# Filling the gap in front of a block's fourth channel with a convolution piece and six down matmuls

## What is computed

```python
def reference(x, itok, ...):            # x: (B=128, C=32, L=512)
    y = irfft(rfft(x, 2 * L) * rfft(K, 2 * L))[..., :L] + x * D[:, None]   # K: one kernel of length L per channel
    y = y * (arange(L) < length)                                           # mask
    q = fp8(clip(y / in_scale, -448, 448))
    hidden = silu(q @ gate_w.T * s) * (q @ up_w.T * s)                     # I = 1376
    return x + fp8(clip(hidden / down_scale)) @ down_w.T * s
```

## Time and profile before

| | us |
|---|---|
| median of 3 runs (lowest, highest) | 334.01 (332.64, 334.09) |
| the profiled execution, its own time | 333.13 |
| its span in the profile | 331.4 |
| PE busy | 310.4 (94%) |
| DVE busy | 304.5 (92%) |
| ACT busy | 205.4 (62%) |

### The profile page before, as it was taken

One profiled execution on the slowest core, in us unless ns is written; L12 is line 12 of the kernel. 1 busy time (PEld: TensorE's weight loads), 2 busy tenths in 40 slices (PEclk: granted clock), 3 DMA queues, 4 the chain that ended last, 5 costly groups with the idle time before them and its releaser, 6 DMA issues.

```text
span 331.4 us, 4869 instructions
## 1 busy us (share of the span) xinstructions
PE 310.4 (94%) x1591; PEld 163.6 (49%) x1591; DVE 304.5 (92%) x470; ACT 205.4 (62%) x312; POOL 13.0 (4%) x20
## 2 busy tenths in 40 slices
PE   0879898879999999999999999999999999989996
PEld 0746554445546454555546454555546454434443
DVE  5989899999999899998999899998999899997784
ACT  2457778366764958475764957475764958544540
POOL 2022000000001000010000000010001000010010
PEclk9999999999999999999999999999999999999999
DMA  6559999500000782046600791046600760070027
GB/s 240 101 165 216 236 289 370 197 1 2 0 0 0 130 287 93 2 74 207 225 0 0 127 342 38 0 79 205 224 0 1 130 253 0 0 129 0 0 37 220
DMA packets 13794, 38.27 MB, mean 115 GB/s; under 512 B 1392, under 2 KB 6352, under 8 KB 10832
## 3 DMA queue, kind: packets, MB, share of 16 engines
q1 hardware_dynamic: 8192, 26.48, 22.5%
q0 software_dynamic: 5584, 11.57, 20.0%
HBM read 33.80 MB, written 15.81 MB: 150 GB/s over the span
## 4 chain that ended last, share of the span: by engine, by line
PE 81%; DVE 12%; issue 2%; DMA 2%; ACT 2%; DVEq 0%; SPq 0%
PE gate_ps L490 20%; PE up_ps L490 20%; PE down_ps L456 19%; PE y_ps L441 17%; DVE yt L773 2%; DVE hv L800 2%; DVE ht L808 2%; PE y_ps L423 2%; DVE hq L817 2%; PE y_ps L534 1%; DVE yq L784 1%; DVE ym L765 1%; PE down_ps L534 1%; DMA toep<-kpad_scratch 1%; DMA prm<-in_params 1%
## 5 line engine op out<-in xcount | busy, mean ns | idle before, releaser
L366 ACT ACTIVATE sil<-gate_ps,fac 128x512 f32<-128x512 f32 (+1 forms) x88 | 60.1, 685 | 86.8 <-PE gate_ps L490 86.5
L490 PE MATMUL gate_ps<-yq,wg 128*128 128x512 bf16 (+2 forms) x372 | 89.5, 363 | 5.9 <-DVE yq L791 2.9
L490 PE MATMUL up_ps<-yq,wu 128*128 128x512 bf16 (+2 forms) x372 | 89.5, 363 | 0.0
L441 PE MATMUL y_ps<-xt,toep 128*128 128x512 f32 (+3 forms) x256 | 80.7, 435 | 0.7 <-DMA toep<-kpad_scratch 0.7
L800 DVE SCALAR_TENSOR_TENSOR hv<-up_ps,fac,sil 128x512 f32<-128x512 f32 (+1 forms) x88 | 65.6, 746 | 15.7 <-ACT sil L366 11.5
L456 PE MATMUL down_ps<-wd,hq 128*128 128x512 bf16 (+1 forms) x308 | 79.2, 379 | 0.3 <-DVE hq L825 0.3
L490 PEld LDWEIGHTS gate_ps<-yq,wg 128*128 128x128 bf16 x372 | 35.8, 100 | 48.5 <-issue 4.6
L441 PEld LDWEIGHTS y_ps<-xt,toep 128*128 128x128 f32 x256 | 47.0, 190 | 21.1 <-issue 2.9
L490 PEld LDWEIGHTS up_ps<-yq,wu 128*128 128x128 bf16 x372 | 36.3, 100 | 38.3
L808 DVE SCALAR_TENSOR_TENSOR ht<-hc,hv 128x1024 f32<-128x1024 f32 (+1 forms) x48 | 54.1, 1127 | 0.0
L817 DVE SCALAR_TENSOR_TENSOR hq<-hc,ht 128x1024 bf16<-128x1024 f32 (+1 forms) x48 | 54.1, 1126 | 0.0
(11 more groups left out here) (139 smaller groups left out, 110.7 us busy)
## 6 DMA issues: line engine op xcount, KB each, us to landing
xt<-in_xT SPq DMA_DIRECT2D x8, 1024.0 KB, 7.4
toep<-kpad_scratch SPq DMA_DIRECT2D x7, 1024.0 KB, 9.7
out<-in_x SPq DMA_DIRECT2D x7, 1024.0 KB, 5.7
out<-res POOLq DMA_DIRECT2D x7, 1024.0 KB, 8.0
wd<-in_down POOLq DMA_DIRECT2D x1, 1280.0 KB, 25.3
toep<-kpad_scratch SPq DMA_DIRECT2D x4, 256.0 KB, 3.7
xt<-in_x SPq DMA_DIRECT2D x1, 1024.0 KB, 7.2
out<-xt SPq DMA_DIRECT2D x3, 256.0 KB, 3.2
```

Of the source, the lines that this page charges most:

```text
L366: nc.scalar.activation(sil[b][0:w, :], gate_ps[b][0:w, :], ACT.Silu, scale=fac[0:w, S_GATE:S_GATE + 1]).then_inc(silu_done, 1)
L441: last = nc.tensor.matmul(y_ps[h % 2][:, d * P:L], toep[par][:, h, d * P:(d + 1) * P], xt[par][:, h, 0:L - d * P], start=(d == 0), stop=(d ...
L490: mm = nc.tensor.matmul(ps[b][0:w, cols], wt[:, k, c * P:c * P + w], yq[par][:, version, k, cols], start=(k == 0), stop=(k == LB - 1))
```

## The change

In slot 0 the convolution piece (channel 1 of the next block, distance 2) and the down matmuls now stand between the first three channels' gate and up and the fourth's. Slot 0 issues six down matmuls in place of four; slots 1 to 8 four each, slots 9 and 10 three each. The list of DVE, of ACT and of the DMA queues is unchanged.

```diff
-                for s in range(HB * c, HB * (c + 1)):
+                for s in range(DOWN_PLAN[c], DOWN_PLAN[c + 1]):
...
+            def conv_part(g, par, half, c, down, ahead):
+
+                for step, h, distances in CONV_PLAN.get(c, ()):
+                    if step <= ahead and (down or (step, h) != (1, 1)):
+                        conv(g + step, (par + step) % 2, half + (1 if step == 2 else par), h, distances)
...
                         for lo, hi in (((0, HB - 1), (HB - 1, HB)) if c == 0 else ((0, HB),)):
+                            if c == 0 and hi == HB:
+                                conv_part(g, par, half, c, down, ahead)
+                                if down:
+                                    down_part(g - 1, 1 - par, c)
                             if c == 0:
                                 at_least(pe, yq_ready, HB * g + hi)
...
-                    for step, h, distances in CONV_PLAN.get(c, ()):
-                        if step <= ahead and (down or (step, h) != (1, 1)):
-                            conv(g + step, (par + step) % 2, half + (1 if step == 2 else par), h, distances)
-                    if down:
+                    if c or not down:
+                        conv_part(g, par, half, c, down, ahead)
+                    if c and down:
                         down_part(g - 1, 1 - par, c)
...
+DOWN_PLAN = [0, 6, 10, 14, 18, 22, 26, 30, 34, 38, 41, 44]
```

## The result

The change made the kernel slower, and by more than forecast: 359.49 us median (6 runs, 357.37 to 362.22) against 333.44 us (6 runs, 332.39 to 334.10), a ratio of 1.079 (95% interval 1.073 to 1.085), where 349.3 us and a range of 343 to 354 had been forecast. The profiled execution took 358.24 us, with a span of 356.6.

The account below looks back on a forecast made before the run. PE was taken as the bound, DVE close behind. New waits for pair 4's clip, summed over blocks 1 to 7, added 16.2 us to the profiled 333.13 us, giving 349.3 us, range 343 to 354.

Parts of the forecast that it names:

- What bounds the kernel, and that two waits for `yq` were to be gained: PE bounds the kernel; gate's two waits for `yq`, in blocks 1 and 7, could be filled, worth up to 2.9 us.
- The fourth channel 1.79 us late, the product and the clips with it: Block 2, slot 0: fourth channel starts at 108.59, not 106.80; DVE's product moves to 109.92, pair 4's clip to 114.18.
- The wait for pair 4 in slot 1: k = 8, moved from slot 2 to slot 1, waits for DVE's clip of pair 4: 2.60 us in block 2.
- The lower bound, DVE not delayed, 340.8 us: Rival: clip not delayed, k = 8 waits 0.81 us, blocks 2 to 6 cost 4.5 us; chance 0.10.
- by the row at 1.67 us each wait costs only itself: PE ran at full clock after block 1's 1.67 us wait, so new waits were taken to slow no matmuls.
- half rate after 9.13 us: At the start, PE's first matmuls after 9.13 us idle took 5.31 us, 1.78 ns a column.
- The rule of the Trainium skill named there: Idle gaps between bursts of matmuls can put PE's clock back to half each time, slowing the matmuls behind each wait.
- The chance of 0.06: Chance given to the rival that PE's clock falls after each wait, 368 us in all.
- that rival: PE's clock falls after each of seven waits, 2.65 us each, 18.6 us, 368 us in all; chance 0.06.
- reads full in every slice: PE's granted clock row showed full clock throughout the kernel before, although its first matmuls ran slowly.

Follow-up runs that it names:

- the order alone: Changed kernel with four down matmuls in every slot, new order of slot 0 kept, k = 8 in slot 2: 331.53 us, ratio 0.994 to the kernel before.
- the wait filled: Changed kernel with 11 more matmuls of 512 columns right before k = 8 in each block, result overwritten: 349.92 us, ratio 1.049 to the kernel before.
- the plan alone: Changed kernel with convolution piece and down matmuls back behind the fourth channel, changed DOWN_PLAN kept: 341.95 us, ratio 1.023 to the kernel before.
- the order alone's second measurement: Same kernel again, new order of slot 0 with four down matmuls in every slot: 331.92 us, ratio 0.995 to the kernel before.

## Why the prediction was wrong

- *What bounds the kernel, and that two waits for `yq` were to be gained:* right. Both vanished, and the order alone gained 1.2 us.
- *The fourth channel 1.79 us late, the product and the clips with it:* right. In block 2 the product started 4.36 us after the block's start (112.28 in the trace after), 1.73 later than in the earlier trace rows, the clips at 116.54, 8.62 after it where they had been at 6.89.
- *The wait for pair 4 in slot 1:* right in place and size. 2.44 us against 2.60, 2.25 against 2.41, 3.05 against 3.3, seven waits of 17.7 us in all where some 19 were forecast. Its consequences were forecast at 16.2 us and came to 15.9 in the kernel with the wait filled, right block by block. (Its median of 349.92 us next to the forecast 349.3 is closer than it should be read: three of its four runs hold a half-clock stretch, and the one at full clock took 348.76.)
- *The lower bound, DVE not delayed, 340.8 us:* measured with the plan alone, 340.26 us at full clock.
- **The step that failed** is "by the row at 1.67 us each wait costs only itself". The full clock behind a wait of 1.67 us was carried to waits of 2.4 to 3.3 us, beyond the only row that spoke for it, and so the sum held the clock at nothing. The other row, half rate after 9.13 us, lay far on the other side. Behind six of the seven waits the clock fell to half, and PE's matmuls took 9.9 us more. The rule of the Trainium skill named there ("TensorE: Matmul & The Clock Gate", "HAM oscillation — how this bites in real kernels") was the better guide, and the trace agrees with it in six of seven blocks, though all but one of these gaps are shorter than the waits for DMA of about 3 to 5 us in the page's example. The chance of 0.06 was far too small.
- *The price of that rival* was off the other way: 2.65 us a wait, 18.6 in all, from one stretch of 5.31 us at the start. It cost 1.63 us a stretch, the mean of the table's rest over the six blocks with half clock, 9.8 us in all. The mean granted clock says the same: 0.971 over 356.6 us is 10.3 us of full clock lost.
- *The granted clock "reads full in every slice":* the row does, but it is no evidence for the start. The first matmuls took 1.78 ns a column under a row that says 1.00, and in the changed kernel, under the same row, the same fourteen took 4.27 us in place of 5.31. The row cannot be relied on there.
- *The spread:* the changed kernel's six runs had mean clocks of 0.976, 0.971, 0.971, 0.966, 0.962 and 0.962 for 357.37, 358.24, 358.68, 360.29, 361.39 and 362.22 us, five to eight stretches of 0.005 each by their means (only the run of 358.24 us has a trace, with six). The forecast's range had no such term.

## What to carry to other kernels

When filler work is pulled forward into a gap, look at what the last pieces of the list then stand in front of: here one number of a plan (10, where 8 costs nothing) put two matmuls ahead of the clip of their operand, and held up an in-order engine with everything behind them. If an engine runs at 94% and another at 92%, as here, a result that gets later on the first can come back as a wait through the second; whether it does depends on how soon the first needs it, as the order alone shows. A new wait on PE of two microseconds or more is to be priced with its clock, not by its length alone; and where no row of the trace lies near its length, the range has to hold both answers.

## What the runs showed of the hardware

The granted clock took two levels, 1.00 and 0.50. In the dense stream of blocks 1 to 7, stretches of 0.50 followed waits: in the changed kernel's profiled execution behind six of seven waits of 2.25 to 3.05 us, in two others behind waits of 1.97 and 2.04 us, in none behind one of 1.92 or behind those of 1.71 us and less. The same wait of 2.44 us was followed by half clock in blocks 2 and 3 and by full clock in block 4 of one execution. Each such stretch cost about 1.6 us. Adding 77 matmuls into the waits made the kernel 9.6 us faster.

The length of the wait alone does not settle it, and at the start of the kernel the limit of the blocks does not hold. A wait of 3.24 us for `toep` was followed by full clock (the plan alone), one of 2.28 us in the order alone's second measurement by half clock, where eight convolution matmuls took 3.49 us in place of 2.38:

```profile
33.20 3.49 PE L441 MATMUL y_ps<-xt,toep 128*128 128x512 f32 x8 [2.28 <-DMA toep<-kpad_scratch]
```

And in seven of the ten experiments' profiled executions the clock fell to half at 19.3 to 20.7 us and rose again at 22.7 to 24.2, and between PE's first matmuls and this stretch no wait was longer than 1.6 us; in the kernel before, in the changed kernel and in the other three experiments it was full there after waits of nearly the same lengths. What decides between them stays open. Runs of the kernel before with a mean clock of 0.995 were 13 of 18, 6 of 23 and 14 of 23 in three groups, which is most of what splits its times into some 332.5 and some 334.2 us; where its stretch lies no trace shows, since its one profiled execution ran at full clock.
